# Four post-norm sub-layers on one core: new tables of step times, and a last stage whose logarithms and outputs change places

## Time and profile before

| what | value |
|---|---|
| median of 3 runs | 1890.19 us |
| profiled execution, its own time | 1891.06 us |
| its span | 1888.9 us |
| PE busy | 1565.9 us (83%), 12169 instructions |
| DVE busy | 1253.5 us (66%) |
| POOL busy | 1120.1 us (59%), of it gathers 1117.2 us (1056 of them) |
| ACT busy | 946.2 us (50%) |
| DMA | 178.74 MB, mean 95 GB/s |
| granted clock, mean | 0.92 |

### The profile page before, as it was taken

The page is one execution under the profiler, slowest core; times in us unless marked ns, Lnnn a source line. Parts: engine busy times, 40 slices in busy tenths (PEclk is TensorE's granted clock), DMA queues, the critical chain, the costliest instruction groups (busy, mean ns, idle before and its releaser), DMA issues. The chain is left out here.

```text
span 1888.9 us, 31819 instructions
## 1 busy us (share of the span) xinstructions
PE 1565.9 (83%) x12169; PEld 1066.5 (56%) x12177; DVE 1253.5 (66%) x2161; ACT 946.2 (50%) x2333; POOL 1120.1 (59%) x1069
## 2 busy tenths in 40 slices
PE   5778888778889987778889877879997689999866
PEld 3455554546556655455566454656664357677535
DVE  7576664687777857777778577777875444454345
ACT  3266567334646654356466543554664244444333
POOL 0000002777777757777777577777775777777700
PEclk8899999899998989998989988999998899899966
DMA  4010012334433444344333443444335533333311
GB/s 166 4 37 18 18 24 44 111 99 129 120 104 112 116 84 112 98 128 120 104 110 115 85 111 95 118 115 117 109 112 96 174 109 98 109 96 101 105 18 45
DMA packets 93421, 178.74 MB, mean 95 GB/s; under 512 B 21452, under 2 KB 50264, under 8 KB 93016
## 3 DMA queue, kind: packets, MB, share of 16 engines
q0 software_dynamic: 50688, 138.48, 27.2%
q1 hardware_dynamic: 42584, 38.23, 6.9%
HBM read 151.46 MB, written 9.44 MB: 85 GB/s over the span
## 5 line engine op out<-in xcount | busy, mean ns | idle before, releaser
L760 POOL DMA_INDIRECT pool_c<-rows_of_x,idx x1056 | 1117.2, 1058 | 677.9 <-issue 351.3
L1279 DVE TENSOR_TENSOR pool_c<-pool_c 128x768 f32<-128x768 f32 x352 | 333.8, 953 | 151.5 <-DMA pool_c<-rows_of_x,idx 150.8
L1667 PE MATMUL c<-ident,pool_c 128*128 128x128 f32 x2112 | 308.4, 286 | 74.7 <-DVE pool_c L1279 74.5
L1667 PEld LDWEIGHTS c<-ident,pool_c 128*128 128x128 f32 x2112 | 253.5, 147 | 160.1 <-DVE pool_c L1279 96.4
L891 ACT ACTIVATE prob<-sc,nmax 128x128 f32<-128x128 f32 x512 | 179.3, 374 | 0.2
L802 ACT COPY pool_a<-tb 128x512 f32<-128x512 f32 x188 | 112.9, 600 | 35.6 <-PE tb L1433 29.0
L891 ACT ACTIVATION_READ_ACCUMULATOR prob<-sc,nmax 128x1 f32 x512 | 110.0, 215 | 0.0
L1175 DVE TENSOR_REDUCE ssq<-pool_a 128x16 f32<-128x1024 f32 x64 | 77.7, 1215 | 31.2 <-ACT pool_a L867 31.2
L1597 PE MATMUL ta<-vmix,pool_a 128*64 128x64 f32 x1024 | 71.9, 224 | 26.0 <-ACT pool_a L802 26.0
L1597 PEld LDWEIGHTS ta<-vmix,pool_a 128*64 128x64 f32 x1024 | 64.5, 138 | 45.2 <-issue 45.2
L1571 PE MATMUL ta<-ident,pool_a 128*128 128x128 f32 x512 | 73.1, 289 | 12.9 <-DVE pool_a L1198 11.6
(11 more groups left out here) (467 smaller groups left out, 3194.8 us busy)
## 6 DMA issues: line engine op xcount, KB each, us to landing
pool_c<-rows_of_x,idx POOLq DMA_INDIRECT x1056
vmix<-vring SPq DMA_DIRECT2D x128, 128.0 KB
rows_of_x<-x2tok SPq DMA_DIRECT2D x16, 256.0 KB
xtok<-in_x SPq DMA_DIRECT2D x4, 512.0 KB
x_of_all<-x2tok SPq DMA_DIRECT2D x8, 256.0 KB, 3.2
out<-pool_c SPq DMA_DIRECT2D x8, 256.0 KB, 2.3
wqkv<-in_wqkv SPq DMA_DIRECT2D x1, 1536.0 KB
xtok<-x_of_all SPq DMA_DIRECT2D x3, 512.0 KB, 4.6
```

The lines of the kernel that those rows point to most:

```text
L760: pool.indirect_dma_start(gat[:, n % GB, s, :], None, tables[b % 2], bass.IndirectOffsetOnAxis(ap=idx[:, t, SC * c + s:SC * c + s + 1], ax ...
L1279: V.tensor_tensor(g4, g4, wv, ALU.mult).then_inc(SEM["c_prod"], 1)
L1667: ins = mm(out[:, c:c + P], x, ident[:], start=(i == 0 and k == 0), stop=(i == BCH - 1 and k == len(parts) - 1), is_transpose=True, skip_g ...
```

## The change

Every table of times gets new numbers. The steps themselves are the same, none more and none less; only their order on PE, ACT and DVE changes, and with it the banks that `plan` deals. In the last stage OUT_A gives four of batch 2's eight output tiles to DVE, ACT's logs of batch g are issued in front of ACT's output tiles of batch g-1, and DVE's `final_norm(2)` with its outputs is issued in front of `final_stats(3)`. In the kernel after, lines behind these edits stand 6 lines further down (from the last stage of ACT on) and 8 (behind the last stage of DVE, so all of PE).

```diff
-SECOND_AT = (0.0, 27.61, 55.22, 82.75)
-TAIL_AT = 23.47
+SECOND_AT = (0.0, 27.61, 55.22, 82.74)
+TAIL_AT = 23.13
 TILE_AT = (
-    (0.0, 1.0, 2.0, 3.0, 4.1, 5.0, 6.02, 7.0, 9.0, 10.01, 11.01, 12.01, 13.01, 14.01, 15.01, 16.01),
+    (0.0, 1.0, 2.0, 2.99, 4.09, 4.99, 6.01, 6.99, 9.0, 10.01, 11.01, 12.01, 13.01, 14.01, 15.01, 15.97),
...
-OUT_A = (T, T, T, TB)
+OUT_A = (T, T, TB, TB)
...
+            def final_out(g):
+
+                act.wait_ge(last["newton"], 5 * (g + 1))
+                for t in range(OUT_A[g]):
...
             for g in range(B):
                 ts = slice(T * g, T * (g + 1))
                 act.wait_ge(last["bn"], 2 * T * (g + 1))
                 nc.scalar.activation(frs[:, 0, ts], fmv[:, ts, 1], ACT.Ln, bias=col(EPS)).then_inc(last["rstd"], 1)
                 act.wait_ge(last["rstd"], 2 * g + 1)
                 nc.scalar.activation(frs[:, 1, ts], frs[:, 0, ts], ACT.Exp, scale=-0.5).then_inc(last["rstd"], 1)
-                act.wait_ge(last["newton"], 5 * (g + 1))
-                for t in range(OUT_A[g]):
...
+                if g:
+                    final_out(g - 1)
+            final_out(B - 1)
...
-            for g in range(B):
+            final_stats(0)
+            for g in range(1, B - 1):
                 final_stats(g)
-                if g:
-                    final_norm(g - 1)
+                final_norm(g - 1)
+            final_norm(B - 2)
+            final_stats(B - 1)
             final_norm(B - 1)
```

More of the change, by code:

```diff
@@ L984, in _ @@
             run(act, first, second, moe, "act")
+            def final_out(g):
+                act.wait_ge(last["newton"], 5 * (g + 1))
+                for t in range(OUT_A[g]):
+                    i = T * g + t
+                    nc.scalar.activation(fin[:, i, :], final_psum(i // TB)[:, P * (t % TB):P * (t % TB + 1)], ACT.Identity, bias=fnb[:, i:i + 1],
+                                         scale=frs[:, 1, i:i + 1]).then_inc(last["out_a"], 1)
             for g in range(B):
@@ L990, in _ @@
                 nc.scalar.activation(frs[:, 1, ts], frs[:, 0, ts], ACT.Exp, scale=-0.5).then_inc(last["rstd"], 1)
-                act.wait_ge(last["newton"], 5 * (g + 1))
-                for t in range(OUT_A[g]):
-                    i = T * g + t
-                    nc.scalar.activation(fin[:, i, :], final_psum(i // TB)[:, P * (t % TB):P * (t % TB + 1)], ACT.Identity, bias=fnb[:, i:i + 1],
-                                         scale=frs[:, 1, i:i + 1]).then_inc(last["out_a"], 1)
+                if g:
+                    final_out(g - 1)
+            final_out(B - 1)
         @block.vector
```

## The result

| | before | after |
|---|---|---|
| median, us (runs) | 1890.29 (4) | 1876.96 (4) |
| range of the runs, us | 1887.31 to 1892.72 | 1876.42 to 1878.53 |
| ratio | | 0.9927, 95% interval 0.9909 to 0.9944 |
| span of the profiled execution, us | 1888.9 | 1876.5 |
| gathers busy on POOL, us | 1117.2 | 1114.4 |

The account below looks back on a forecast made before the run. POOL's gathers were taken to bound the kernel: first gather, four stretches, three switches, tail. Terms -0.9 - 0.6 - 0.5 + 0.3 - 2.6 = -4.3 took 1891.06 to 1886.8, less 0.87 for 1885.9; range 1881.5 to 1890.5.

Parts of the forecast that it names:

- stretches of gathers: Four stretches of 264 POOL gathers each; pauses in them put at +0.3 us, held gathers at 0.
- First gather, opening: Batch 0's opening: `var` 1 ahead of the first tile's projection brings the tile's rotation 0.9 us earlier.
- First gather, second layer: Batch 0's second layer: fewer ACT table loads around the gates let `down` start 0.6 us earlier.
- Switches: Between batches' gathers: transposes at the first switch start sooner, -0.5 us (bounds 0 and -1.2); other switches 0.
- Pauses: POOL's waits inside batches 0 and 1's gathers: +0.3 us for both, bounds -1.2 and +2.1.
- forecast pause at chunk 69: Batches 0 and 1: POOL waits 1.1 to 1.4 us for PE's accumulation, with the usual 0.30 at chunk 70.
- slower rival: PE falls behind at chunks 62 to 64: 5.7 us more, 1891.6, or 1898 at the lower clock; chance 0.07.
- Tail: Last stage: earlier logs and shared output tiles end 3.1 us sooner, 0.5 back for bunched stores: -2.6 us.
- Stretching of gathers: Gathers lengthened beside DVE operations: 0 us, as the total of DVE operations is the same; 3 either way.
- All gains arrive: Rival: loads, opening, first switch, both pauses and tail gain in full, -9.2 us, some 1881.0; chance 0.20.
- the table loads: ACT's two saved loads around batch 0's second-layer gates, counted in full at -2.56 us in the all-gains rival.
- the holding's 3 us either way: Bound on the gathers' stretching term of 0, from a spread of 3.1 us over three batches.

Follow-up runs that it names:

- e1: Kernel before with only the last stage's edits, all tables of times old: 1885.0 us, ratio 0.9982 to the kernel before.
- e7: Kernel before with two new PE phases alone (output projection before next layer's first scores, scores before chunk 62's accumulation): 1890.93 us, 0.9997.
- e12: Kernel before with new times for the first parts of batches 1 and 2 alone: 1885.01 us, ratio 0.9977.
- e10: e6 plus scores' phase back, ACT's batch 2 outputs before batch 3's logs, rotation's first operation in two halves: 1864.61 us, 0.9875 to before.
- e5: Changed kernel with each weighting in two halves, the second waiting on a semaphore: 1858.23 us, ratio 0.9829 to the kernel before.
- e6: Changed kernel with each weighting in two halves, no wait between them: 1863.47 us, ratio 0.9852 to the kernel before.
- e11: e6 plus scores' phase back, ACT's batch 2 outputs before batch 3's logs, weighting in three parts: 1865.09 us, 0.9859 to before.

## Why the prediction was wrong

The forecast was -4.3, the result -13. What bounds the kernel was read rightly: the sum over first gather, stretches, switches and tail accounts for the result. Two terms failed. The stretches of gathers, pauses and holding together, were put at +0.3 and measure -5.2 by the table of pieces, most of it holding that had been put at nothing; and the first gather, put at -1.5, measures -3.5. The steps:

- *First gather, opening: -0.9, measured -1.95* in the two profiled traces (84.55 against 86.50), and -2.8 by the means of six traces with the old order and five with the new. The mechanism was as told, the size was not: `var`'s place ahead of the projections delayed the rotation's inputs by 0.86 (83.06 + 0.68 against 82.88), where the hand replay had let it and what follows eat 2.7 of the 3.6.
- *First gather, second layer: -0.6, measured -0.84* (rotation of the last tile to first gather 41.2 in all six traces with the old order, 40.4 in all five with the new). Right. With both, the first gather moves 3.5 and not 1.5; single traces had hidden it, since the profiled execution of before had the earliest first gather of six with that order.
- *Switches: -0.5, measured -1.1 in sum.* The number is near by luck, for the mechanism is not shown. The 1.2 of the transposes' wait went whole, but it went in e1 too, whose order is the old one: the first switch goes with the clock of `down`, and no trace shows it shortened by the order.
- *Pauses: +0.3.* The profiled execution shows none, -1.2. The forecast pause at chunk 69 exists (2.74 in e7, 1.1 in e12), but only with `down` at the lower clock. The working took the 4.46 of the earlier trace rows as the duration of `down` and did not ask what the sum becomes at 2.8, where the accumulation comes 1.6 sooner. Its slower rival counted the lower clock as a further cost, though the `down` that set its slack of 0.46 already stood at it.
- *Tail: -2.6, measured -3.0* for the last stage with its stores. The mechanism and its size were right, and so was the 0.5 for the stores. The other 3 us of the tail are the granted clock in the experts' steps, which varies between executions of the same order and was no term of the sum.
- *Stretching of gathers: 0, measured* -4.4 in batches 0 to 2 and +0.5 in batch 3, by the means of POOL's busy time over three to six traces each. This is the step that failed outright: the total of DVE operations was the argument for nothing, but what counts is which operation runs when a gather starts. Of the 4.4, 2.2 are the order's doing: the gathers at chunks 85 and 86 of batches 0 and 1. Whether it causes the rest is not settled: the same order moves by 1.6 to 1.9 a batch between executions, and batch 2's old and new values overlap.

"All gains arrive" (-9.2, 0.20) was nearest, by its total and not by its terms: the table loads gave 0.84 and not 2.56, the pauses and the switch went with the clock, the opening stood in it at 1.1 and not at 2.8, and the holding not at all. The range was too narrow on the fast side because the profiled execution was taken as the kernel: the spread of 11 us between executions of before was in no bound, and the holding's 3 us either way came from three batches of one execution.

The rule of the Trainium skill, GPSIMD Engine Reference, section 1 (Specifications), that GpSimd and VectorE contend where a VectorE instruction has two SBUF inputs, is borne out: the weightings and the rotation, which held gathers for 91 of 116 us, are of that kind, and halving the weightings took 28 to 34 us off POOL. In the trace of before 48 gathers began beside L1175, a reduction over one SBUF tile, with up to 1.21 us of it left, and 49 beside L1228, which has one input in PSUM; none of them was held. The rule names no price; these runs do.

## What to carry to other kernels

Where one engine's queue sets the time, ask what other engine's operation runs at the moment each of its instructions starts. Here a holding was at most the rest of one operation in most cases, and making that operation shorter cut it (28 to 34 us); moving it cut little (1.1 a batch), and a holding can pass to the operation behind, as the rotation showed in e10. A sum of terms from one profiled execution needs the spread between executions as a bound of its own; identical code here differed by 2 us in a stretch of 360. And a duration of a TensorE instruction taken from one trace belongs to a clock level: redo the sum at the other level, since the pauses, the first switch and the tail here went with it.

## What the runs showed of the hardware

- A gather's issue on POOL is held by a two-input DVE operation that is already running, until about 0.13 before its end, and not by one that starts behind it while DVE was idle (rows above). With weightings of 0.95 the holding was 68.6 us in a run; with halves of 0.55 it is 47 in e5 and 45 in e6, with thirds 35 in e11.
- Two weightings that began 0.38 behind a gather's start held it on, where another DVE operation ran at that start: 3.01. Halves without a wait between them gained as much as halves with one, and 5 of 84 gathers were held through both.
- The granted clock of a given matmul differs between executions of the same code: batch 1's `down` of the earlier trace rows took 4.46 in before and 2.82 in e1. Over fourteen traces, batches 0 and 1 each, it took 2.8 in 9 cases and 4.4 to 4.5 in 19, and POOL paused behind it in none of the 9 and in 16 of the 19.
